# Graph attention and expert layer on one core: who fetches the 128th source row of every chunk of edges

## The chip, the core and the metric

The kernel runs on one core of one Trainium2 chip. Its engines are TensorE (PE, with its weight loads shown apart as PEld), VectorE (DVE), ScalarE (ACT), GpSimd (POOL) and SyncE (SP); SP only waits, loads registers and issues DMAs. The metric is the time of the whole program on the device in microseconds (us), as the median of a few runs.

## The reference, cut to what matters

6250 nodes with 256 features, 206,250 edges sorted by destination. A graph attention layer is followed by a mixture of 16 experts, of which two are chosen per node. The change touches only the part that works edge by edge:

```python
z = einsum('ni,hid->nhd', h, W)                  # 4 heads of 64
e = leaky_relu(es[src] + ed[dst])                # one number per edge and head
ex = exp(e - m[dst])
alpha = ex / segment_sum(ex, dst)[dst]
out = segment_sum(alpha[:, :, None] * z[src], dst)
x = x + out;  x = x + moe(layernorm(x))
```

For each edge the row `z[src]` must be fetched: 256 values and 4 scores `es`, 260 floats or 1040 bytes.

## The kernel before, in words

A first stage writes `z_table` (one row of 260 floats per node) to HBM. The edge stage then goes through the edges in **chunks** of 128 (one edge per partition) and **groups** of `G = 4` chunks: 403 groups. A group lies in one slot of `ring`, which has `RING = 4` slots. A **visit** is a pair of a group and a tile of 128 destination nodes that occurs in it. There are 451 visits, 48 more than groups, so 48 groups have two visits and 355 have one.

- **GpSimd** (`gather`) waits for a group until its slot is free, then issues one indirect DMA per chunk: 128 rows of `z_table`, chosen by a column of `src_idx`, into the 128 partitions of the slot. "Free" means that VectorE has made the message of the last visit of the group four before: `pool.wait_ge(b_msg, done + 1)`, where `group_free` holds the number `done` for each group.
- **SyncE** goes through the groups in order. `relay(g, ...)` waits until group g has landed and raises `b_group` by one; only then may ScalarE open the group. For odd g `replace_pair` loads two more rows of destination numbers (`dst_bc`), and for even g `relay_pair` passes on that such a pair has landed. In the time that is left SyncE gathers whole chunks by itself: `fetch_row` loads one index into a register and copies one row of `z_table` into `side`, 4 rows after an even group and 3 after an odd one (`HAND_ROWS`); when 128 are there, `place_side` copies them into the ring. In this way 10 chunks of 1612 come past GpSimd, which issues 1602 gathers.
- **ScalarE** copies the scores out of the ring when the group is released (`es_edge`, in `open_group`), and makes the exponents.
- **VectorE** makes arguments, one-hot matrices and messages, in an order written out by hand. The number behind each piece says how many visits it lags:

```python
written_out(VISITS, SR, [(e_sum, AHEAD), (look_up, AHEAD + 1), (e_add, AHEAD), (make_ST, 0), (e_lrelu, AHEAD),
                         (accumulate, AHEAD + 1 + MSG_TO_ACC), (e_shift, AHEAD), (one_hot, AHEAD + 1),
                         (e_clamp, AHEAD), (message, AHEAD + 1), (finish, None)], steps=FINISH)
```

In one step VectorE therefore begins visit v with `e_add`, which needs `es_edge` of visit v, and at the end of the same step makes the message of visit v - 1 (`message`, which reads the ring and raises `b_msg`).
- **TensorE** multiplies messages with the one-hot matrices and sums them by destination.

All waits of an engine block what is queued behind them on that engine.

Of the kernel before, what the change touches and what calls it, by code (L numbers as in the profile page):

```python
# [35 lines left out]
P = 128  # L36
G = 4
RING = 4
# [15 lines left out]
ZR = 12  # L54
SOON = AHEAD + 1
SLACK = 4
HAND_ROWS = (4, 3)
LADDER = 4


# [51 lines left out]
def gnn_moe_kernel(nc, E, x, x_turned, src_cols, dst_cols, dst_flat, dst_last, W, a_src, a_dst, gate_w, gate_b, w1, b1, w2, b2, gamma, beta, out):  # L112
    N, D = out.shape
    HEADS, DH = a_src.shape
    EXPERTS, _, F = w1.shape
    TOP = 2
    NT = -(-N // P)
# [3 lines left out]
    ROW = D + HEADS  # L121
    CHUNKS = -(-E // P)
    GROUPS = -(-CHUNKS // G)
# [14 lines left out]
    z_table = nc.dram_tensor("z_table", [NT * P, ROW], F32).ap()  # L138
# [19 lines left out]
    with whole:  # L158
# [27 lines left out]
        src_idx = sb(graph, "src_idx", [P, BLOCKS * P], I32)  # L186
# [381 lines left out]
        b_landed = [sem(f"b_landed{i}") for i in range(RING)]  # L568
        b_over = sem("b_over"); b_go = sem("b_go")
        b_pstep = sem("b_pstep"); b_nodes = sem("b_nodes")  # L570
        b_group = sem("b_group")
        PAIRED, PAIRS = ROWS // 2, -(-GROUPS // 2)
        b_side = [sem(f"b_side{i}") for i in range(2)]; b_placed = sem("b_placed")
        b_dst = [sem(f"b_dst{i}") for i in range(PAIRED)]; b_rows = sem("b_rows")
        b_S = sem("b_S"); b_ST = sem("b_ST")
        b_dest = sem("b_dest"); b_estep = sem("b_estep"); b_arg = sem("b_arg"); b_p = sem("b_p")
# [22 lines left out]
        for batches in SPANS:  # L599
            at = range(BATCHES[batches[0]].start, BATCHES[batches[-1]].stop)  # L600
            assert at.start // KEPT == (at.stop - 1) // KEPT
        SH = 2 * HEADS
        PER_PASS = (b_pstep, b_nodes, b_group, *b_side, b_placed, *b_dst, b_rows, b_S, b_ST, b_dest, b_estep, b_arg, b_p, b_msg, b_sum, b_acc, b_es, b_fstep, b_reset, b_rden,
                    b_scaled, b_added, b_stats, b_var, b_root, b_ready, b_xn, b_xT_ps, b_xT, b_log_ps, b_log, *b_saved)
        assert sorted(one.num for one in PER_PASS) == list(range(b_pstep.num, b_saved[-1].num + 1))
        PASS_STEPS = 11
        HAND_GROUPS, brought, hand_rows = [], 0, {}
        for g in range(GROUPS - RING):
            hand_rows[g] = [divmod(brought + u, P) for u in range(HAND_ROWS[g % 2])]
            brought += HAND_ROWS[g % 2]  # L610
            if brought // P > len(HAND_GROUPS):
                HAND_GROUPS.append(g + RING)
        BY_HAND = {g: m for m, g in enumerate(HAND_GROUPS)}
        THIRDS = 3
        SPAN_TILES = [range(BATCHES[batches[0]].start, BATCHES[batches[-1]].stop) for batches in SPANS]
        PAIRED_SPANS = sum(len(batches) == 2 for batches in SPANS)
# [7 lines left out]
        with ExitStack() as ctx:  # L624
# [12 lines left out]
            earg = sb(ctx, "earg", [P, 4, 3, G * HEADS])  # L637
            msg = sb(ctx, "msg", [P, MR, G, ROW])
            nodes_rest = msg[:, 0, :, :].rearrange("p g c -> p (g c)")[:, 0:NT * SH].rearrange("p (t c) -> p t c", c=SH)
            side = sb(ctx, "side", [P, 2, ROW])  # L640
            psE = [ps(ctx, f"psEb{i}") for i in range(SR // BANKED)]
            psM = [ps(ctx, f"psMb{i}") for i in range(2)]
            psP = [ps(ctx, f"psPb{i}") for i in range(2)]
# [16 lines left out]
            @block.sync  # L660
            def _(sp):
                npass = sp.value_load(npass_i[0:1, 0:1], min_val=1, max_val=PASSES_MAX)
                with sp.Fori(0, npass) as k:
                    def gathered(s, upto):
                        return sum(G - (h in BY_HAND) for h in range(s, upto, RING))

                    def relay(g, s, r):

                        sp.wait_ge(b_landed[s], 16 * (k * gathered(s, GROUPS) + gathered(s, g + 1)))
                        if g in BY_HAND:  # L670
                            sp.wait_ge(b_placed, 16 * (BY_HAND[g] + 1))
                        sp.nop().then_inc(b_group, 1)  # L672

                    def load_pair(g, at):
                        sp.dma_start(dst_bc[:, 2 * at:2 * at + 2, :].rearrange("p o f -> p (o f)"),
                                     over(dst_rows[bass.ds(g * (G * P), 2 * G * P)].unsqueeze(0), [P, 2 * G * P])).then_inc(b_dst[at], 16)

                    def replace_pair(g, at):

                        done = sp.value_load(group_free[0:1, g + 1 - ROWS + RING:g + 2 - ROWS + RING], min_val=1, max_val=VISITS)  # L680
                        sp.wait_ge(b_ST, done)
                        load_pair(g, at)

                    def relay_pair(at, r):
                        sp.wait_ge(b_dst[at], 16 * (r + 1))
                        sp.nop().then_inc(b_rows, 1)
                    def fetch_row(m, p):

                        chunk = HAND_GROUPS[m] * G + G - 1
                        row = sp.value_load(src_idx[p:p + 1, chunk:chunk + 1]).with_bounds(min_val=0, max_val=NT * P - 1)  # L690
                        sp.dma_start(side[p:p + 1, m % 2, :], z_table[bass.ds(row, 1), :]).then_inc(b_side[m % 2], 16)

                    def place_side(g, m):

                        sp.wait_ge(b_side[m % 2], 16 * P * (m // 2 + 1))
                        done = sp.value_load(group_free[0:1, g:g + 1], min_val=0, max_val=VISITS)
                        sp.wait_ge(b_msg, done + 1)
                        sp.dma_start(ring[:, g % RING, G - 1, :], side[:, m % 2, :]).then_inc(b_placed, 16)
                    for at in range(PAIRED):
                        load_pair(2 * at, at)  # L700
                    for at in range(PAIRED - 1):
                        relay_pair(at, 0)

                    for g in range(GROUPS):
                        pair = g // 2 + PAIRED - 1
                        if g % 2 == 0 and pair < PAIRS:
                            relay_pair(pair % PAIRED, pair // PAIRED)
                        relay(g, g % RING, g // RING)
                        if g % 2 and g // 2 + PAIRED < PAIRS:
                            replace_pair(g + ROWS - 1, g // 2 % PAIRED)  # L710
                        if g + 2 in BY_HAND:
                            place_side(g + 2, BY_HAND[g + 2])
                        for m, p in hand_rows.get(g, ()):
                            if m < len(HAND_GROUPS):
                                fetch_row(m, p)

                    for at in range(PAIRED):
                        sp.wait_ge(b_dst[at], 16 * len(range(at, PAIRS, PAIRED)))
                    for i in range(2):
                        sp.wait_ge(b_side[i], 16 * P * len(range(i, len(HAND_GROUPS), 2)))  # L720
                    sp.wait_ge(b_placed, 16 * len(HAND_GROUPS))
                    for done, total in ((b_group, GROUPS), (b_rows, PAIRS), (b_S, VISITS), (b_ST, VISITS), (b_dest, VISITS), (b_estep, 4 * VISITS),
                                        (b_arg, VISITS), (b_p, VISITS), (b_msg, VISITS + 1), (b_sum, VISITS), (b_acc, VISITS), (b_es, VISITS),
                                        (b_fstep, FIN_STEPS), (b_reset, NT), (b_rden, NB), (b_scaled, NT), (b_added, NT), (b_stats, NT), (b_var, len(SPANS)),
                                        (b_root, len(SPANS)), (b_ready, len(SPANS)), (b_xn, NT), (b_xT_ps, NT), (b_xT, NT), (b_log_ps, NT), (b_log, NT),
                                        *((b_saved[i], 16 * len(range(i, NT, XN))) for i in range(XN)), (b_pstep, PASS_STEPS), (b_nodes, 1)):
                        sp.wait_ge(done, total)
                    sp.wait_ge(b_over, 4 * k + 4)
                    sp.sem_inc(apart, 1)
                    sp.sem_clear(range(b_pstep.num, b_saved[-1].num + 1))  # L730
                    sp.sem_inc(b_go, 1)

            @block.gpsimd
            def _(pool):
                npass = pool.value_load(npass_i[0:1, 0:1], min_val=1, max_val=PASSES_MAX)
                with pool.Fori(0, npass) as k:
                    def gather(g, s, r):

                        done = pool.value_load(group_free[0:1, bass.ds(g, 1)], min_val=0, max_val=VISITS)
                        pool.wait_ge(b_msg, done + 1)  # L740
                        pool.sem_inc(apart, 1)
                        for c in range(G - 1 if g in BY_HAND else G):
                            at = src_idx[:, g * G + c:g * G + c + 1]
                            nc.gpsimd.indirect_dma_start(ring[:, s, c, :], None, z_table,  # L744
                                                         bass.IndirectOffsetOnAxis(ap=at, axis=0)).then_inc(b_landed[s], 16)
                    for g in range(GROUPS):
                        gather(g, g % RING, g // RING)
                    pool.drain()
                    pool.sem_inc(b_over, 1)
                    pool.wait_ge(b_go, k + 1)  # L750
# [817 lines left out]
```

## Time and profile before

| | us |
|---|---|
| median of 3 runs (2661.21 to 2662.76) | 2661.33 |
| span of the profiled execution, first to last instruction | 2659.8 |
| median of the runs less that span | 1.5 |
| first release of a group to the last (403 releases) | 88.5 to 2094.5 |
| first gather of the edge stage to the last (1602) | 81.5 to 2091.3 |

The profiled execution has no time of its own apart from its span; 1.5 us is what the median of the runs is longer. The edge stage takes about three quarters of the span. In the rows below "L744" is line 744 of the kernel before, a letter q behind an engine ("SPq") is its instruction queue, and the idle time of a group of instructions is that of its engine just before them, with what ended it.

### The profile page before, as it was taken

The numbers are of one execution on the slowest core, as the hardware profiler recorded it, in microseconds if no ns is written. First come the engines' busy times: TensorE is split into PE (matmuls) and PEld (weight loads), VectorE is DVE, ScalarE is ACT, GpSimd is POOL, SyncE is SP. The second block draws the span as 40 slices with busy tenths as digits, with TensorE's granted clock in tenths as the row PEclk, the third lists the DMA queues.
The fourth block names the chain that finished last, engine by engine and source line by source line (L and its number), as shares of the span: only waits on it lengthen the run. The fifth ranks groups of instructions, "written<-read, shape, count | busy, mean of one in ns | idle before, by whom it ended". The sixth has DMA issues, their size and how long they took to land. (4 is left out here: it accounts for less than half of the span.)

```text
span 2659.8 us, 56988 instructions
## 1 busy us (share of the span) xinstructions
PE 1833.5 (69%) x9023; PEld 1427.5 (54%) x9024; DVE 1783.6 (67%) x5444; ACT 783.4 (29%) x3130; POOL 1810.8 (68%) x1943
## 2 busy tenths in 40 slices
PE   7566766665666666666666666666665449999987
PEld 5344544444454454445444444444454339999985
DVE  6577777777786777767777777676777774333326
ACT  4434112212121221122121212111222235555557
POOL 0577777777777777777777777777777345555547
PEclk9688787888887887878788887887888769999998
DMA  9454545555455554455445555554555328433328
GB/s 318 143 136 132 138 136 140 142 136 140 139 141 138 136 144 136 133 144 140 133 137 142 138 138 139 138 140 134 140 141 138 86 64 248 153 105 108 106 96 282
DMA packets 186615, 380.07 MB, mean 143 GB/s; under 512 B 40053, under 2 KB 90656, under 8 KB 185930
## 3 DMA queue, kind: packets, MB, share of 16 engines
q0 software_dynamic: 87264, 241.69, 33.2%
q1 hardware_dynamic: 76152, 114.56, 14.0%
q10 hardware_dynamic: 22898, 20.85, 2.8%
q14 instruction: 239, 1.96, 0.2%
q8 instruction: 62, 1.02, 0.2%
HBM read 341.68 MB, written 33.93 MB: 141 GB/s over the span
## 5 line engine op out<-in xcount | busy, mean ns | idle before, releaser
L744 POOL DMA_INDIRECT ring<-z_table,src_idx x1602 | 1518.8, 948 | 497.6 <-issue 475.7
L1032 PE MATMUL psMb<-msg,S 128*128 128x260 f32 x3608 | 1183.7, 484 | 529.2 <-DVE msg L904 528.7
L1032 PEld LDWEIGHTS psMb<-msg,S 128*128 128x128 f32 x3608 | 812.4, 236 | 712.4 <-DVE msg L904 571.0
L904 DVE TENSOR_TENSOR msg<-ring,psPb 128x1024 f32<-128x1024 f32 x451 | 546.1, 1211 | 0.0
L952 ACT COPY es_edge<-ring 128x16 f32 x451 | 91.5, 203 | 1387.1 <-SPq L672 1347.5
L816 DVE TENSOR_TENSOR earg<-es_edge,dest_sum 128x16 f32<-128x16 f32 x451 | 80.5, 178 | 380.8 <-ACT es_edge L952 346.4
L804 DVE TENSOR_TENSOR S<-iota_f,psPb 128x512 f32<-128x512 f32 x451 | 306.2, 679 | 1.7 <-ACT psPb L961 1.6
L1021 PEld LDWEIGHTS psEb<-node_thirds,ST 128*128 128x128 bf16 x1804 | 104.6, 105 | 322.9 <-issue 300.0
L798 DVE TENSOR_SCALAR ST<-dst_bc,iota_p 128x512 bf16 x451 | 170.6, 378 | 130.5 <-issue 124.4
L1021 PE MATMUL psEb<-node_thirds,ST 128*128 x1804 | 120.8, 179 | 187.7 <-DVE earg L833 96.1
L1396 DVE COPY xT<-psXd 128x256 f32<-128x256 f32 x108 | 45.9, 425 | 263.9 <-PE psXd L1330 263.9
L1308 POOL DMA_INDIRECT rows_sb<-norm_rows,src_sb x108 | 108.2, 1002 | 161.4 <-DVE src_sb L1385 145.5
L1340 PE MATMUL psHd<-xT,w_sb 128*128 128x128 f32 x1728 | 212.5, 277 | 0.0
L1352 PE MATMUL psYd<-w_all,hid 128*128 x864 | 204.3, 379 | 0.3 <-ACT hid L1375 0.3
L1340 PEld LDWEIGHTS psHd<-xT,w_sb 128*128 128x128 f32 x1728 | 203.5, 193 | 0.1
L921 DVE TENSOR_TENSOR acc<-acc,psMb 128x260 f32 x451 | 190.9, 423 | 8.6 <-issue 5.2
L1352 PEld LDWEIGHTS psYd<-w_all,hid 128*128 128x128 f32 x864 | 155.9, 190 | 17.3 <-issue 0.5
L1363 ACT COPY w_sb<-w_all 128x1024 f32 x108 | 112.8, 1045 | 151.2 <-PE psHd L1340 129.8
L1315 POOL DMA_INDIRECT pair_rows<-y_sb,dst_sb x108 | 106.7, 988 | 45.6 <-issue 33.8
L1375 ACT ACTIVATE hid<-psHd,b1T 128x128 f32<-128x128 f32 x432 | 123.6, 368 | 30.2 <-issue 26.2
L941 ACT ACTIVATE psPb<-dst_col,visit_base 128x4 f32 x451 | 120.3, 267 | 1.6 <-issue 1.6
L810 DVE TENSOR_REDUCE dest_sum<-psEb 128x32 f32<-128x96 f32 x451 | 111.8, 248 | 2.2 <-DVE shift_b L882 1.1
(214 smaller groups left out, 1578.7 us busy)
## 6 DMA issues: line engine op xcount, KB each, us to landing
dst_bc<-dst_rows SPq DMA_DIRECT2D x202, 256.0 KB, 3.4
ring<-z_table,src_idx POOLq DMA_INDIRECT x1602
side<-z_table SPq DMA_DIRECT2D x1280, 1.0 KB
w_all<-in_L_ffn_w_dram SPq DMA_DIRECT2D x32, 512.0 KB, 5.4
b_sb<-in_L_ffn_b_dram ACTq DMA_DIRECT2D x108, 128.0 KB, 3.1
got<-pair_rows SPq DMA_DIRECT2D x48, 256.0 KB, 4.1
z_table<-z_out SPq DMA_DIRECT2D x49, 130.0 KB, 6.3
norm_rows<-xnb ACTq DMA_DIRECT2D x49, 128.0 KB, 2.6
```

The source lines that it names most:

```text
L744: nc.gpsimd.indirect_dma_start(ring[:, s, c, :], None, z_table, bass.IndirectOffsetOnAxis(ap=at, axis=0)).then_inc(b_landed[s], 16)
L798: nc.vector.tensor_scalar(ST[:, s % MR, :], dst_bc[:, bass.ds(slot, 1), :].rearrange("p o f -> p (o f)"), iota_p[:, 0:1], None, ALU.is_equ ...
L804: nc.vector.tensor_tensor(S[:, s % MR, :, :], over(iota_f[:, 0:P].unsqueeze(1), [P, G, P]), over(psP[s % 2][:, G * HEADS:G * HEADS + G].un ...
L904: nc.vector.tensor_tensor(msg[:, s % MR, :, 0:D].rearrange("p g (h d) -> p g h d", h=HEADS), ring[:, bass.ds(slot, 1), :, 0:D].rearrange(" ...
L921: nc.vector.tensor_tensor(at, at, psM[s % 2][:, 0:ROW], ALU.add).then_inc(b_acc, 1)
L941: nc.scalar.activation(psP[s % 2][:, G * HEADS:G * HEADS + G], dst_col[:, bass.ds(group * G, G)], ACT.Identity, bias=visit_base[:, v:v + 1])
L1021: last = nc.tensor.matmul(dest_of(s)[:, c * THIRDS * SH:(c + 1) * THIRDS * SH], ST[:, s % MR, c * P:(c + 1) * P], node_thirds[:, bass.ds(t ...
L1032: last = nc.tensor.matmul(psM[s % 2][:, 0:ROW], S[:, s % MR, c, :], msg[:, s % MR, c, :], start=c == 0, stop=c == G - 1)
L1340: last = nc.tensor.matmul(psH[s % 2][:, f * P:(f + 1) * P], w1_sb[:, s % 2, c, f * P:(f + 1) * P], xT[:, s % 2, c, :], start=c == 0, stop= ...
L1352: last = nc.tensor.matmul(psY[s % 2][:, 0:D], hid[:, s % 2, f, :], w2_f, start=f == 0, stop=f == FC - 1)
L1363: nc.scalar.copy(w1_sb[:, s % 2, :, :].rearrange("p c f -> p (c f)"), w_all[:, bass.ds(e, 1), 0:KD * F].rearrange("p o f -> p (o f)")).the ...
L1375: last = nc.scalar.activation(hid[:, s % 2, f, :], psH[s % 2][:, f * P:(f + 1) * P], ACT.Relu, bias=b1T[:, bass.ds(e, 1), f:f + 1].rearran ...
```

## The change

GpSimd now gathers the first 127 rows of every chunk and SyncE copies the last row of every chunk straight into partition 127 of the ring. For that, `bring_rows(g, s)` loads the four indices of a group with one register load, waits for the slot as GpSimd does, and issues four DMAs of one row each. It is called for groups 0 to 2 ahead of the loop and for group g + 3 behind the release of group g. The buffer `side`, `fetch_row`, `place_side` and the ten chunks brought by hand are gone, so GpSimd issues all 1612 gathers. The release of a group now waits for both.

```diff
-HAND_ROWS = (4, 3)
+TAKEN = P - 1
...
                     def relay(g, s, r):
-                        sp.wait_ge(b_landed[s], 16 * (k * gathered(s, GROUPS) + gathered(s, g + 1)))
-                        if g in BY_HAND:
-                            sp.wait_ge(b_placed, 16 * (BY_HAND[g] + 1))
+                        sp.wait_ge(b_landed[s], 16 * G * (k * len(range(s, GROUPS, RING)) + r + 1))
+                        sp.wait_ge(b_brought[s], 16 * G * (r + 1))
                         sp.nop().then_inc(b_group, 1)
...
-                    def fetch_row(m, p):
-                        chunk = HAND_GROUPS[m] * G + G - 1
-                        row = sp.value_load(src_idx[p:p + 1, chunk:chunk + 1]).with_bounds(min_val=0, max_val=NT * P - 1)
-                        sp.dma_start(side[p:p + 1, m % 2, :], z_table[bass.ds(row, 1), :]).then_inc(b_side[m % 2], 16)
-                    def place_side(g, m):
-                        sp.wait_ge(b_side[m % 2], 16 * P * (m // 2 + 1))
+                    def bring_rows(g, s):
                         done = sp.value_load(group_free[0:1, g:g + 1], min_val=0, max_val=VISITS)
+                        _, loaded = nc.values_load_multi_w_load_instructions(src_idx[TAKEN:P, g * G:(g + 1) * G], engines=[mybir.EngineType.SP])
+                        rows = [row.with_bounds(min_val=0, max_val=NT * P - 1) for row in loaded]
                         sp.wait_ge(b_msg, done + 1)
-                        sp.dma_start(ring[:, g % RING, G - 1, :], side[:, m % 2, :]).then_inc(b_placed, 16)
+                        for c in range(G):
+                            sp.dma_start(ring[TAKEN:P, s, c, :], z_table[bass.ds(rows[c], 1), :]).then_inc(b_brought[s], 16)
...
+                    for g in range(RING - 1):
+                        bring_rows(g, g)
                     for g in range(GROUPS):
...
                         relay(g, g % RING, g // RING)
                         if g % 2 and g // 2 + PAIRED < PAIRS:
                             replace_pair(g + ROWS - 1, g // 2 % PAIRED)
-                        if g + 2 in BY_HAND:
-                            place_side(g + 2, BY_HAND[g + 2])
-                        for m, p in hand_rows.get(g, ()):
-                            if m < len(HAND_GROUPS):
-                                fetch_row(m, p)
+                        if g + RING - 1 < GROUPS:
+                            bring_rows(g + RING - 1, (g + RING - 1) % RING)
...
-                        for c in range(G - 1 if g in BY_HAND else G):
-                            at = src_idx[:, g * G + c:g * G + c + 1]
-                            nc.gpsimd.indirect_dma_start(ring[:, s, c, :], None, z_table,
+                        for c in range(G):
+                            at = src_idx[0:TAKEN, g * G + c:g * G + c + 1]
+                            nc.gpsimd.indirect_dma_start(ring[0:TAKEN, s, c, :], None, z_table,
                                                          bass.IndirectOffsetOnAxis(ap=at, axis=0)).then_inc(b_landed[s], 16)
```

On SyncE, this is what stood behind the release of an odd group early in the edge stage: register arithmetic for the release (L669), the load of a pair of destination rows (L680, L675), and then one register load (L690) and one DMA (L691) for each row brought by hand, of which the first two of three are shown.

```order
L669 ISA
L680 TENSOR_LOAD group_free
L680 ISA x2
L675 DMA dst_bc<-dst_rows 128x1024
L690 TENSOR_LOAD src_idx
L691 ISA
L691 DMA side<-z_table 1x260
L690 TENSOR_LOAD src_idx
L691 ISA
L691 DMA side<-z_table 1x260
```

Now the same place reads as follows: L668 and L663 are the pair of destination rows, L678 loads the number that frees the slot, L679 loads four indices, the first L683 carries the wait for the message, and a DMA of one row follows each L683 (two of four are shown).

```order
L668 TENSOR_LOAD group_free
L668 ISA x2
L663 DMA dst_bc<-dst_rows 128x1024
L678 TENSOR_LOAD group_free
L678 ISA x2
L679 TENSOR_LOAD src_idx
L681 REGISTER_ALU
L683 ISA
L683 DMA ring<-z_table 1x260
L683 ISA
L683 DMA ring<-z_table 1x260
```

Three register loads for indices have become one, the copies go to the ring and not to the side buffer, and a wait on VectorE's messages now stands on SyncE between the release of one group and the release of the next.

On GpSimd a group was, in its wait for the slot (L739, L740) and its gathers (L744):

```order
L739 TENSOR_LOAD group_free
L739 ISA x2
L740 REGISTER_ALU
L744 DMA ring<-z_table,src_idx 128x260 x4
```

and is now:

```order
L722 TENSOR_LOAD group_free
L722 ISA x2
L723 REGISTER_ALU
L727 DMA ring<-z_table,src_idx 127x260 x4
```

Nothing moved there; the gathers have 127 partitions in place of 128, and the ten groups that had three gathers have four.

## Rows read from the trace of the kernel before

**Rows 1.** The page: busy time of each engine, share of span, instructions.
```profile
PE 1833.5 (69%) x9023; PEld 1427.5 (54%) x9024; DVE 1783.6 (67%) x5444; ACT 783.4 (29%) x3130; POOL 1810.8 (68%) x1943
```

**Rows 2.** Busy time by engine in the edge stage, granted clock, DMA share, GB/s.
```profile
90.00:2090.00 2000.00, 1286.70 (x5648) 949.52 (x5648) 1475.27 (x4373) 432.62 (x2282) 1510.25 (x1594) 0.82 0.51 138
```

**Rows 3.** Groups by line: busy us, mean ns, then idle before and releasers.
```profile
L744 POOL DMA_INDIRECT ring<-z_table,src_idx x1602 | 1518.8, 948 | 497.6 <-issue 475.7 <-DVE msg L904 21.9
...
L952 ACT COPY es_edge<-ring 128x16 f32 x451 | 91.5, 203 | 1387.1 <-SPq L672 1347.5
```

**Rows 4.** Who waited for whom: us in total, times, longest.
```profile
ACT es_edge L952 <- SPq L672: 1347.5, 375, 6.5
...
POOL ring L744 <- DVE msg L904: 21.9, 68, 0.9
```

**Rows 5.** SyncE's own waits, same columns.
```profile
SPq L672 <- DMA ring<-z_table,src_idx: 385.9, 357, 5.4
```

**Rows 6.** Single lines: ns min/median/max, first and last start; the last near 1006 us.
```profile
L744 POOL DMA_INDIRECT ring<-z_table,src_idx x1602: 940/946/1382, 81.5 to 2091.3; - x178
...
L904 DVE TENSOR_TENSOR msg<-ring,psPb x451: 1204/1212/1217, 96.5 to 2098.7; 128x1024 f32<-128x1024 f32 x151
...
L672 SPq EVENT_SEMAPHORE  x403: 17/17/28, 88.5 to 2094.5; - x135
...
L672 SPq EVENT_SEMAPHORE  x1: 17/17/17, 1006.3 to 1006.3; - x1
```

**Rows 7.** Timeline from 1000 to 1016 us: start, us, engine, line, idle before.
```profile
1000.52 1.21 DVE L904 TENSOR_TENSOR msg<-ring,psPb 128x1024 f32<-128x1024 f32 x1
...
1004.05 1.22 DVE L904 TENSOR_TENSOR msg<-ring,psPb 128x1024 f32<-128x1024 f32 x1
...
1006.47 0.20 ACT L952 COPY es_edge<-ring 128x16 f32 x1 [4.71 <-SPq L672]
...
1008.13 3.15 SPq L691 DMA_DIRECT2D side<-z_table  x4
...
1008.68 1.21 DVE L904 TENSOR_TENSOR msg<-ring,psPb 128x1024 f32<-128x1024 f32 x1
...
1010.93 0.95 POOL L744 DMA_INDIRECT ring<-z_table,src_idx  x1 [0.30 <-issue]
1011.62 0.20 ACT L952 COPY es_edge<-ring 128x16 f32 x1 [2.51 <-SPq L672]
...
1012.18 0.95 POOL L744 DMA_INDIRECT ring<-z_table,src_idx  x1 [0.30 <-issue]
1012.22 0.35 SPq L675 DMA_DIRECT2D dst_bc<-dst_rows  x1
...
1013.91 1.21 DVE L904 TENSOR_TENSOR msg<-ring,psPb 128x1024 f32<-128x1024 f32 x1
```

**Rows 8.** SyncE's instructions for one row by hand: ns min/median/max, first and last.
```profile
L690 SPq TENSOR_LOAD <-src_idx x1280: 267/499/782, 88.5 to 1910.9; - x183
...
L691 SPq FUSED_REGOPS  x1280: 37/37/47, 88.9 to 1911.5; - x183
L691 SPq MOVE side<-z_table x1280: 29/29/40, 88.9 to 1911.6; - x183
L691 SPq DMA_DIRECT2D side<-z_table x1280: 254/258/327, 89.0 to 1911.6; - x183
```

**Rows 9.** GpSimd's DMA queue (packets, MB, share of 16 engines); its other users.
```profile
q0 software_dynamic: 87264, 241.69, 33.2%
...
L1308 POOL DMA_INDIRECT rows_sb<-norm_rows,src_sb x108 | 108.2, 1002 | 161.4 <-DVE src_sb L1385 145.5
...
L1315 POOL DMA_INDIRECT pair_rows<-y_sb,dst_sb x108 | 106.7, 988 | 45.6 <-issue 33.8
```

**Rows 10.** Timeline at the start of the edge stage: SyncE's DMAs back to back.
```profile
79.64 1.75 SPq L675 DMA_DIRECT2D dst_bc<-dst_rows  x4
```

**Rows 11.** DMA issues by line: KB each, median us to landing.
```profile
dst_bc<-dst_rows SPq DMA_DIRECT2D x202, 256.0 KB, 3.4
```

More of the change, by code:

```diff
@@ L572, in gnn_moe_kernel @@
         PAIRED, PAIRS = ROWS // 2, -(-GROUPS // 2)
-        b_side = [sem(f"b_side{i}") for i in range(2)]; b_placed = sem("b_placed")
+        b_brought = [sem(f"b_brought{i}") for i in range(RING)]
         b_dst = [sem(f"b_dst{i}") for i in range(PAIRED)]; b_rows = sem("b_rows")
@@ L602, in gnn_moe_kernel @@
         SH = 2 * HEADS
-        PER_PASS = (b_pstep, b_nodes, b_group, *b_side, b_placed, *b_dst, b_rows, b_S, b_ST, b_dest, b_estep, b_arg, b_p, b_msg, b_sum, b_acc, b_es, b_fstep, b_reset, b_rden,
+        PER_PASS = (b_pstep, b_nodes, b_group, *b_brought, *b_dst, b_rows, b_S, b_ST, b_dest, b_estep, b_arg, b_p, b_msg, b_sum, b_acc, b_es, b_fstep, b_reset, b_rden,
                     b_scaled, b_added, b_stats, b_var, b_root, b_ready, b_xn, b_xT_ps, b_xT, b_log_ps, b_log, *b_saved)
@@ L606, in gnn_moe_kernel @@
         PASS_STEPS = 11
[L607 to L613, printed above, removed]
         THIRDS = 3
@@ L639, in gnn_moe_kernel @@
             nodes_rest = msg[:, 0, :, :].rearrange("p g c -> p (g c)")[:, 0:NT * SH].rearrange("p (t c) -> p t c", c=SH)
-            side = sb(ctx, "side", [P, 2, ROW])
             psE = [ps(ctx, f"psEb{i}") for i in range(SR // BANKED)]
@@ L663, in _ @@
                 with sp.Fori(0, npass) as k:
-                    def gathered(s, upto):
-                        return sum(G - (h in BY_HAND) for h in range(s, upto, RING))
                     def relay(g, s, r):
-                        sp.wait_ge(b_landed[s], 16 * (k * gathered(s, GROUPS) + gathered(s, g + 1)))
-                        if g in BY_HAND:
-                            sp.wait_ge(b_placed, 16 * (BY_HAND[g] + 1))
+                        sp.wait_ge(b_landed[s], 16 * G * (k * len(range(s, GROUPS, RING)) + r + 1))
+                        sp.wait_ge(b_brought[s], 16 * G * (r + 1))
                         sp.nop().then_inc(b_group, 1)
@@ L710, in _ @@
                             replace_pair(g + ROWS - 1, g // 2 % PAIRED)
-                        if g + 2 in BY_HAND:
-                            place_side(g + 2, BY_HAND[g + 2])
-                        for m, p in hand_rows.get(g, ()):
-                            if m < len(HAND_GROUPS):
-                                fetch_row(m, p)
+                        if g + RING - 1 < GROUPS:
+                            bring_rows(g + RING - 1, (g + RING - 1) % RING)
                     for at in range(PAIRED):
                         sp.wait_ge(b_dst[at], 16 * len(range(at, PAIRS, PAIRED)))
-                    for i in range(2):
-                        sp.wait_ge(b_side[i], 16 * P * len(range(i, len(HAND_GROUPS), 2)))
-                    sp.wait_ge(b_placed, 16 * len(HAND_GROUPS))
+                    for s in range(RING):
+                        sp.wait_ge(b_brought[s], 16 * G * len(range(s, GROUPS, RING)))
                     for done, total in ((b_group, GROUPS), (b_rows, PAIRS), (b_S, VISITS), (b_ST, VISITS), (b_dest, VISITS), (b_estep, 4 * VISITS),
```

## The prediction

> **What bounds the kernel now.** I read the page first [rows 1]: no engine is busy for more than 69% of the span, so the bound has to be looked for by stage. In the 2000 us of the edge stage [rows 2] GpSimd is busy for 1510 us, VectorE for 1475, TensorE for 1287; DMA engines stand at half. The groups by line [rows 3] then say what GpSimd's remaining time is: 475.7 us of "issue" before 1602 gathers, about 0.30 us each, against only 21.9 us in which it waited for VectorE to free a slot (68 times, [rows 4]). A gather is 0.948 us plus these 0.30, and the timeline shows two of them starting 1.25 us apart with nothing else between them [rows 7]. So GpSimd runs at its own pace: (2091.3 - 81.5) / 1601 = 1.255 us per gather, and the releases keep the same pace, (2094.5 - 88.5) / 402 = 4.99 us per group [rows 6].
>
> Everybody behind it waits: ScalarE spent 1347.5 us waiting for SyncE's release [rows 4], and SyncE in turn 385.9 us for a gather to land [rows 5], about 1 us per group. SyncE is thus idle for only a fifth of each group; it is no bound, but not far from one.
>
> The timeline [rows 7] gives the fact on which my forecast rests. A group is released at 1006.3 [rows 6]; `es_edge` starts at 1006.47; VectorE, which needs it, begins its step, and the message at the end of that step ends at 1008.68 + 1.21 = 1009.89. By the written order this is the message of the *previous* visit, the last one of the group before. Start of `es_edge` to end of message is 3.42 us; for the next group 1011.62 to 1015.12, or 3.50. Hence slot of group g - 1 is freed some 3.6 us **after** group g has been released. For GpSimd this is harmless, since it asks for that slot much later.
>
> **The change, part by part.**
>
> *GpSimd.* Ten gathers more: 10 x 1.255 = 12.6 us if GpSimd stayed the bound. The price of a gather with 127 rows is in no row. Bounds: the three indirect transfers here, all with 128 rows, take 0.948, 0.988 and 1.002 us [rows 3, 9], so I take 0.95, with nothing gained for one row less (one 128th of 0.948 us is 7 ns, or 12 us in all, which would just cancel the ten). How a different row count might change more than this is a rival below.
>
> *Transfers removed.* 1280 rows into `side`, ten copies from it, and their register loads leave SyncE. They stood in the time in which SyncE would have waited for the gathers, so taking them away gains nothing by itself.
>
> *SyncE's new work per group.* Two register loads (0.5 us each by [rows 8]) plus, for odd groups, the pair of destination rows (0.35 us and a load) come right behind the release. That is 1.4 to 2.5 us and is hidden, since the wait that follows ends 3.6 us behind the release. The pair's own wait, on the one-hot matrix of a visit that runs five visits ahead, is long met.
>
> *The new wait.* `bring_rows(g + 3)` stands behind the release of g and waits for the message of the last visit of g - 1. As just read, that message cannot end before about 3.6 us after this very release. Behind the wait on SyncE's queue stand four DMAs and then the release of g + 1, for which ScalarE and VectorE wait. Thus release, score copy, VectorE's step, four DMAs and next release form a closed loop, which runs once per group and does not depend on GpSimd.
>
> *The price of four DMAs.* In before, four rows by hand took 3.15 us from first to last DMA [rows 7]: (3.15 - 0.258) / 3 = 0.964 us per row, of which 0.499 is the load [rows 8]. DMA, arithmetic and move are 0.258 + 0.037 + 0.029 = 0.324; the remaining 0.141 is the hand-over between four instructions, 0.035 each. Without the load a row costs 0.324 + 3 x 0.035 = 0.43, and four cost 1.73 us. Bounds: if arithmetic and move hid under the DMA, 4 x (0.258 + 0.035) = 1.17; if a DMA straight behind another took the 0.35 us of the larger one [rows 7], 4 x (0.35 + 0.17) = 2.1. Four larger ones back to back took 1.75 us [rows 10], which also speaks for the middle.
>
> *The loop.* Release to `es_edge` 1006.3 to 1006.47: 0.17. `es_edge` to end of message: 3.43. Message to SyncE: estimated as 0.10, between nothing and the 0.17 of the other hand-over. Four rows: 1.73. The two waits of the release: 0.10, estimated as three of the 0.035 hand-overs. Sum: 5.53 us, against 4.99 now.
>
> *Groups with two visits.* There VectorE makes one step with no release in front of it and the next while SyncE's four DMAs are already done. Two unstalled messages are 1004.05 - 1000.52 = 3.53 us apart [rows 7], so such a group costs 2 x 3.53 = 7.06 us.
>
> *The stage.* 402 intervals between releases, 48 of them with two visits: 354 x 5.53 + 48 x 7.06 = 1957.6 + 338.9 = 2296.5 us. Before: 2094.5 - 88.5 = 2006.0. Difference +290.5. Ahead of the loop SyncE brings three groups, each about two loads with their hand-overs and four rows, 1.0 + 0.2 + 1.73 = 2.9 us. It does so behind three pairs of destination rows, the third of which is issued at some 80.9 [rows 10] and lands 3.4 us later [rows 11]: 84.3 + 8.7 = 93.0 for the first release in place of 88.5, +5. Nothing behind the stage changes. The profiled execution would have 2659.8 + 296 = 2956 us; the median of the runs lies 1.5 above its span, which gives **2957**.
>
> *A rule against 127 rows.* Rows first: GpSimd's queue had its packets on the engines for 33.2% of 16 engines' span [rows 9]. Over 1602 + 108 + 108 transfers that is 0.332 x 16 x 2659.8 / 1818 = 7.8 us of one engine per transfer, or 0.49 us if 16 share it. The Trainium skill, DMA: Bandwidth & Descriptors, section "Why a DMA increments its semaphore by 16 and not by 1", says that a DMA is spread over the largest number up to 16 that divides its slowest dimension, which for 127 partitions is 1, though it also tells of software-issued direct copies on trn2 that were still spread over all 16. By the exception the sum stays as it is. By the rule each gather is one engine's work; no run here shows which holds for an indirect one.
>
> **The rivals.**
>
> 1. *Gathers of 127 rows become the bound.* If each lies on one engine, it lands 7.8 us behind its descriptors. From the freeing of a slot: 3 x 1.255 + 0.95 + 7.8 = 12.5 us until the group is there; the loop wants it at 0.10 + 1.73 + 0.10 + 2 x 5.53 = 13.0 us behind the same point. So even this is just hidden, and from 8.3 us per transfer on it decides. At twice 7.8 us, say because two gathers queue on one engine, three groups take 0.95 + 3.77 + 15.6 + 3.6 = 23.9 us, 8.0 per group, and the kernel 2661 + 402 x (8.0 - 4.99) = 3870. Likewise if a gather with its issue costs GpSimd more than 2296 / 1612 = 1.42 us. Against it: half of the DMA time is free [rows 2]. Chance of a time over 3100: 0.11. (The rule of the Trainium skill named above, DMA: Bandwidth & Descriptors, would bring this about.)
> 2. *The four DMAs cost less back to back,* 1.17 us: the loop is 4.97, the stage 354 x 4.97 + 339 = 2098, the kernel 2661 + 92 + 5 = 2758. For it: only 0.258 us of each row is the DMA [rows 8]. Chance of a time from 2670 to 2800: 0.10, most of it (0.08) at 2740 and above.
> 3. *Faster.* A gather of 127 rows takes a cheaper path through GpSimd and the loop doesn't hold SyncE. If a gather's 0.95 halved, 1612 x (0.47 + 0.30) = 1241 us, and VectorE with 451 x 3.53 = 1592 us would be the bound: 2661 - 2006 + 1592 = 2247. It decides only if four rows cost under 0.91 us: with 48 x 7.06 taken off, 2006 leaves 1667 / 354 = 4.71 us for a loop, less 3.43 + 0.37. Their DMAs alone, 4 x 0.258, are more than that. Chance 0.04, and 0.02 for a time within 0.2%, where the wait costs nothing and the ten gathers and one row less cancel.
>
> **How the numbers follow.** My forecast has 0.73. Its own range takes the bounds of four rows: 1.17 gives 2758; 2.1 gives a loop of 5.90 and 2957 + 354 x 0.37 = 3088; the low end is rival 2, so its own range is 2800 to 3090. The range for all reaches down over most of rival 2 and up to the bound, 2740 to 3100: it leaves out rival 1 (0.11), the rest of rival 2 (0.02) and rival 3 with its neighbour (0.06), 0.19 in all. Faster by over 0.2% (about what a measurement of this kernel tells from no change) 0.04; within 0.2%, 0.02; slower 0.94.
>
> **What would show it.** Right: ScalarE's wait for the release grows to some 1640 us; SyncE waits for VectorE's message behind nearly every release and hardly for a landing; releases are 5.5 us apart, 7 in two-visit groups; GpSimd waits for the message before most groups; a row's DMA starts 0.43 us behind the one before. Wrong: SyncE's wait is still for landing gathers, or a gather takes over 1.1 us (rival 1); rows 0.3 us apart (rival 2); a message that is there when SyncE asks for it (rival 3).

## The result, and the profile after

The changed kernel takes 5268.33 us (median of 4 runs, 5266.59 to 5272.02) against 2662.05 us for the kernel before: a ratio of 1.979, 95% interval 1.977 to 1.982. That is far outside the range of the prediction, in the direction that it gave.

The page of the changed kernel: busy time of the engines, then two of the groups by line (busy us, mean ns, idle before, releasers).

```profile
PE 2328.8 (44%) x9023; PEld 1704.4 (32%) x9024; DVE 1851.6 (35%) x5444; ACT 782.0 (15%) x3130; POOL 4404.6 (84%) x1953
...
L727 POOL DMA_INDIRECT ring<-z_table,src_idx x1612 | 4112.6, 2551 | 503.0 <-issue 480.1
...
L935 ACT COPY es_edge<-ring 128x16 f32 x451 | 91.8, 203 | 4028.9 <-SPq L660 4006.3
```

GpSimd went from 1811 us [rows 1] to 4405, and one line holds all of it: a gather takes 2551 ns in place of 948 [rows 3]. The idle time before it, 0.31 us each, is what it was. The same lines one by one (ns min/median/max, first and last start), with the landing of the gathers' DMAs as the last line of the first view:

```profile
L727 POOL DMA_INDIRECT ring<-z_table,src_idx x1612: 2544/2548/2899, 80.6 to 4687.9; - x180
L683 SPq DMA_DIRECT2D ring<-z_table x1612: 224/228/1426, 85.8 to 4670.1; - x180
...
DMA to landing us min/median/max: 7.8/8.0/11.4
```

```profile
L660 SPq EVENT_SEMAPHORE  x403: 27/28/28, 100.0 to 4698.1; - x135
```

The minimum, 2544 ns, stands next to the median: every gather is slow, not some. Nor is it a queue that has filled up, since the first gather, with none in front of it, is slow already:

```profile
80.59 2.90 POOL L727 DMA_INDIRECT ring<-z_table,src_idx  x1 [5.76 <-issue]
```

From first to last gather there are 1611 x 2.860 = 4607.3 us, where [rows 6] had 2009.8. This is +2597.5; the last release comes 10.2 us after the last gather and not 3.2 (+7.0); the first gather starts 0.9 earlier. Together +2603.6, and the spans differ by 5264.7 - 2659.8 = 2604.9. Nothing else moved the time.

The DMA queue of GpSimd (packets, MB, share of 16 engines) tells what a gather has become:

```profile
q0 software_dynamic: 861504, 253.62, 25.0%
```

Before, 87264 packets [rows 9] were 48 for each of 1818 transfers, 3 per engine if all 16 have the same number. Take 216 later transfers at 48 off: (861504 - 10368) / 1612 = 528 packets for a gather of 127 rows, 33 per engine, although there is one row less to move. The bytes grew by only 5%.

SyncE's own waits (us in total, times, longest):

```profile
SPq L660 <- DMA ring<-z_table,src_idx: 1928.1, 403, 11.4
SPq L683 <- DVE msg L887: 617.4, 399, 4.8
```

SyncE does wait for VectorE's message behind nearly each release, as forecast, but then for each group another 4.8 us for the gathers. The timeline (start, us, engine, line, idle before) shows why the first wait costs nothing here:

```profile
2004.57 2.54 POOL L727 DMA_INDIRECT ring<-z_table,src_idx  x1 [0.30 <-issue]
2007.42 2.55 POOL L727 DMA_INDIRECT ring<-z_table,src_idx  x1 [0.31 <-issue]
2009.68 0.20 ACT L935 COPY es_edge<-ring 128x16 f32 x1 [10.70 <-SPq L660]
...
2010.27 2.55 POOL L727 DMA_INDIRECT ring<-z_table,src_idx  x1 [0.30 <-issue]
...
2011.82 0.99 DVE L816 TENSOR_SCALAR earg<-earg 128x16 f32<-128x16 f32 x1
2011.90 1.21 DVE L887 TENSOR_TENSOR msg<-ring,psPb 128x1024 f32<-128x1024 f32 x1
...
2013.12 2.55 POOL L727 DMA_INDIRECT ring<-z_table,src_idx  x1 [0.30 <-DVE msg L887]
...
2013.29 2.08 SPq L683 DMA_DIRECT2D ring<-z_table  x4
...
2021.44 0.20 ACT L935 COPY es_edge<-ring 128x16 f32 x1 [11.16 <-SPq L660]
```

Gathers stand back to back, 2.85 us apart, four of them 11.4 us. SyncE has its four rows out at 2015.4, some 5.7 us behind the opening of the group at 2009.68, and then waits until 2021 for the next landing.

### The profile page after: what moved, and what is told of

It is laid out like the page before. It is cut to its first block and busy times, and to the rows that moved or that the text cites. A ratio compares the mean times of both kernels' runs of the same rounds, so it can differ in the third digit from the quotient of the medians.

```text
span 5264.7 us, 58524 instructions
## 1 busy us (share of the span) xinstructions
PE 2328.8 (44%) x9023; PEld 1704.4 (32%) x9024; DVE 1851.6 (35%) x5444; ACT 782.0 (15%) x3130; POOL 4404.6 (84%) x1953
## 3 DMA queue, kind: packets, MB, share of 16 engines
q0 software_dynamic: 861504, 253.62, 25.0%
q8 instruction: 62, 1.02, 0.1%
## 5 line engine op out<-in xcount | busy, mean ns | idle before, releaser
L727 POOL DMA_INDIRECT ring<-z_table,src_idx x1612 | 4112.6, 2551 | 503.0 <-issue 480.1
L1015 PE MATMUL psMb<-msg,S 128*128 128x260 f32 x3608 | 1635.8, 631 | 669.6 <-DVE msg L887 668.4
L1015 PEld LDWEIGHTS psMb<-msg,S 128*128 128x128 f32 x3608 | 1096.3, 318 | 954.7 <-DVE msg L887 705.9
L1004 PEld LDWEIGHTS psEb<-node_thirds,ST 128*128 128x128 bf16 x1804 | 88.6, 108 | 2219.2 <-issue 2215.1
L887 DVE TENSOR_TENSOR msg<-ring,psPb 128x1024 f32<-128x1024 f32 x451 | 573.0, 1271 | 0.0
L816 DVE TENSOR_SCALAR earg<-earg 128x16 f32<-128x16 f32 x451 | 508.6, 1128 | 0.0
L781 DVE TENSOR_SCALAR ST<-dst_bc,iota_p 128x512 bf16 x451 | 212.6, 472 | 129.7 <-issue 128.7
L1025 PE MATMUL psTb<-gate,xnTb 128*128 128x16 f32 x196 | 46.1, 354 | 191.4 <-ACT xnTb L985 191.4
L793 DVE TENSOR_REDUCE dest_sum<-psEb 128x32 f32<-128x96 f32 x451 | 128.3, 285 | 2.7 <-DVE shift_b L865 1.3
```

What stands on the lines that cost most here:

```text
L727: nc.gpsimd.indirect_dma_start(ring[0:TAKEN, s, c, :], None, z_table, bass.IndirectOffsetOnAxis(ap=at, axis=0)).then_inc(b_landed[s], 16)
L781: nc.vector.tensor_scalar(ST[:, s % MR, :], dst_bc[:, bass.ds(slot, 1), :].rearrange("p o f -> p (o f)"), iota_p[:, 0:1], None, ALU.is_equ ...
L793: nc.vector.tensor_reduce(dest_sum[:, s % 4, :, :], dest_of(s).rearrange("p (g k c) -> p g c k", g=G, k=THIRDS), AX.X, ALU.add).then_inc(b ...
L816: nc.vector.tensor_scalar(earg[:, s % 4, 0, :], earg[:, s % 4, 2, :], 0.0, None, ALU.min).then_inc(b_arg, 1)
L887: nc.vector.tensor_tensor(msg[:, s % MR, :, 0:D].rearrange("p g (h d) -> p g h d", h=HEADS), ring[:, bass.ds(slot, 1), :, 0:D].rearrange(" ...
L1004: last = nc.tensor.matmul(dest_of(s)[:, c * THIRDS * SH:(c + 1) * THIRDS * SH], ST[:, s % MR, c * P:(c + 1) * P], node_thirds[:, bass.ds(t ...
```

## The experiments

Theory A: a gather of 127 rows is dear by itself, since 127 can't be shared out evenly among the DMA engines. Theory B: SyncE's rows disturb the gathers. Theories C and D, on which counts are dear, stand with the second run. A further question was whether the loop of the forecast exists at all, since the changed kernel hides it. Each of the first five runs has one time, beside 2660.57 us for the kernel before in the first four and 2664.22 in the fifth.

**127 rows alone.** SyncE's part is taken out, on the changed kernel:

```diff
                     def relay(g, s, r):
-                        sp.wait_ge(b_brought[s], 16 * G * (r + 1))
...
-                    for g in range(RING - 1):
-                        bring_rows(g, g)
...
-                        if g + RING - 1 < GROUPS:
-                            bring_rows(g + RING - 1, (g + RING - 1) % RING)
...
             def _(pool):
+                nc.gpsimd.memset(ring[:, :, :, :], 0.0).then_inc(b_zero, 1)
```

> The changed kernel without SyncE's part: GpSimd gathers 127 rows per chunk, nobody fetches the last row (partition 127 of the ring is cleared once and stays zero), so one edge in 128 is left out. Theory A (the gather of 127 rows is dear by itself, because 127 has no divisor that spreads it over the DMA engines): a gather still takes about 2.55 us plus 0.30, 1612 x 2.86 = 4610 us between first and last, and the kernel 5260 to 5275, some 5 us more for the clearing. Theory B (SyncE's single rows, on the same engines and the same ring, slow the gathers): the gather falls back to about 0.95, and the kernel to 2661 + 12.6 + 5 = 2680.

Measured: 5268.67 us. The row of the gathers by line:

```profile
L722 POOL DMA_INDIRECT ring<-z_table,src_idx x1612 | 4116.3, 2554 | 497.5 <-issue 474.3 <-DVE msg L882 23.2
```

2554 ns with no row of SyncE anywhere: B is out. The page's row for GpSimd's queue is the same as that of the changed kernel, so the packets too come with the gathers:

```profile
q0 software_dynamic: 861504, 253.62, 25.0%
```

**The price by row count.** On the kernel of the run above:

```diff
-                            at = src_idx[0:TAKEN, g * G + c:g * G + c + 1]
-                            nc.gpsimd.indirect_dma_start(ring[0:TAKEN, s, c, :], None, z_table,
-                                                         bass.IndirectOffsetOnAxis(ap=at, axis=0)).then_inc(b_landed[s], 16)
+                            kind = (g * G + c) % len(KINDS)
+                            KINDS[kind](g * G + c, ring[:, s, c, :]).then_inc(b_landed[s], 16)
```

> As the run with 127 rows alone, but the chunks take turns with 128, 127, 126, 125, 124, 122, 121, 113, 112 and 64 rows, each count from a line of its own, the rest of the ring zero: it leaves those edges out and measures the price by row count. Theory A (price goes with the rows that the busiest engine gets, n divided by the largest divisor of n up to 16; through 0.946 us at 8 and 2.548 at 127 this is 0.838 + 0.0135 per row): 128 0.95, 127 2.55, 126 (9 rows) 0.96, 125 (25) 1.18, 124 (31) 1.26, 122 (61) 1.66, 121 (11) 0.99, 113 (113) 2.36, 112 (7) 0.93, 64 (4) 0.89; mean 1.37 + 0.30, kernel 2661 - 2010 + 1612 x 1.67 = 3350. Theory C (anything but all 128 partitions is slow): every count but 128 near 2.5, kernel near 5000. Theory D (odd counts are slow, even ones not): 127, 125, 121 and 113 near 2.5, the others at or under 0.95, kernel near 3700.

Measured: 3431.34 us. Groups by line; the lines are 127 rows (L725), 113 (L749), 122 (L741), 124 (L737), 125 (L733), 121 (L745), 126 (L729), 128 (L721), 112 (L753) and 64 (L757):

```profile
L725 POOL DMA_INDIRECT ring<-z_table,src_idx x162 | 412.6, 2547 | 49.4 <-issue 49.4
L749 POOL DMA_INDIRECT ring<-z_table,src_idx x161 | 381.1, 2367 | 49.1 <-issue 49.1
L741 POOL DMA_INDIRECT ring<-z_table,src_idx x161 | 267.6, 1662 | 49.0 <-issue 43.2 <-DVE msg L927 5.8
L737 POOL DMA_INDIRECT ring<-z_table,src_idx x161 | 209.0, 1298 | 54.5 <-issue 50.5 <-DVE msg L927 3.9
L733 POOL DMA_INDIRECT ring<-z_table,src_idx x161 | 194.5, 1208 | 49.0 <-issue 49.0
L745 POOL DMA_INDIRECT ring<-z_table,src_idx x161 | 162.2, 1007 | 52.0 <-issue 51.2 <-DVE msg L927 0.8
L729 POOL DMA_INDIRECT ring<-z_table,src_idx x161 | 158.7, 985 | 49.1 <-issue 45.4 <-DVE msg L927 3.7
L721 POOL DMA_INDIRECT ring<-z_table,src_idx x162 | 156.4, 965 | 88.0 <-DVE msg L927 67.7 <-issue 17.8 <-DVEq L783 2.6
L753 POOL DMA_INDIRECT ring<-z_table,src_idx x161 | 150.3, 933 | 49.1 <-issue 48.8 <-DVE msg L927 0.3
L757 POOL DMA_INDIRECT ring<-z_table,src_idx x161 | 145.8, 905 | 49.1 <-issue 49.1
```

| rows n | largest divisor k up to 16 | n / k | expected, us | measured, us |
|---|---|---|---|---|
| 127 | 1 | 127 | 2.55 | 2.547 |
| 113 | 1 | 113 | 2.36 | 2.367 |
| 122 | 2 | 61 | 1.66 | 1.662 |
| 124 | 4 | 31 | 1.26 | 1.298 |
| 125 | 5 | 25 | 1.18 | 1.208 |
| 121 | 11 | 11 | 0.99 | 1.007 |
| 126 | 14 | 9 | 0.96 | 0.985 |
| 128 | 16 | 8 | 0.95 | 0.965 |
| 112 | 16 | 7 | 0.93 | 0.933 |
| 64 | 16 | 4 | 0.89 | 0.905 |

A holds for all ten within 0.04 us; its line was drawn through 128 and 127, so the other eight are its test. C (anything short of 128) fails with 126, 112 and 64; D (odd counts) with 121, which is odd and cheap, and 122, which is even and dear. The kernel's time came out 81 us over the expected 3350 (whose own sum gives 3343): the gathers' mean is 1.388 us, not 1.37, some 30 us in all, and the idle time before them is 538 us and not 1612 x 0.30 = 484, because 82 us of waits for messages came in, 68 of them before 128.

The Trainium skill, DMA: Bandwidth & Descriptors, section "Why a DMA increments its semaphore by 16 and not by 1", gives that divisor as the number of engines that a DMA runs on; the ten rows agree with it, for an indirect gather, and its exception for some direct copies does not show here. That GpSimd's own time for a gather goes with n / k stands in these rows.

The packets follow n / k too. Suppose that the rows of the busiest engine go four to a packet, that one packet more closes its share, and that each of the 16 engines gets as many packets as the busiest: then a gather makes 16 x (n / k / 4, rounded up, + 1) packets, 48 for 128 rows and 528 for 127. Over the ten counts of this run, with the 10368 packets of the later transfers, that is 302032, and the page has exactly this:

```profile
q0 software_dynamic: 302032, 226.60, 27.8%
```

**Rows beside the ring,** which runs the forecast's loop with gathers of 128 rows:

```diff
-                            sp.dma_start(ring[TAKEN:P, s, c, :], z_table[bass.ds(rows[c], 1), :]).then_inc(b_brought[s], 16)
+                            sp.dma_start(beside[TAKEN - c:P - c, g % (RING - 1), :], z_table[bass.ds(rows[c], 1), :]).then_inc(b_brought[s], 16)
...
-                            at = src_idx[0:TAKEN, g * G + c:g * G + c + 1]
-                            nc.gpsimd.indirect_dma_start(ring[0:TAKEN, s, c, :], None, z_table,
+                            at = src_idx[:, g * G + c:g * G + c + 1]
+                            nc.gpsimd.indirect_dma_start(ring[:, s, c, :], None, z_table,
```

> All 128 rows are gathered by GpSimd as before, and SyncE's four rows per group stay with their wait and their place in the order, but go to a small buffer beside the ring that nobody reads; nothing is left out. It runs the loop of the forecast (release, step of VectorE, four DMAs, next release) without the gathers of 127 rows. If the forecast had the loop right: releases about 5.5 us apart, GpSimd waiting for messages, kernel 2880 to 2990. If the wait costs nothing: ten more gathers alone, 2661 + 12.6 = 2674.

Measured: 2975.55 us. Waits of all engines (two rows) and of SyncE in the edge stage (two), and its releases:

```profile
ACT es_edge L936 <- SPq L661: 1739.6, 390, 6.8
...
POOL ring L728 <- DVE msg L888: 343.1, 299, 3.6
```

```profile
SPq L684 <- DVE msg L888: 818.4, 399, 5.0
...
SPq L661 <- DMA ring<-z_table,src_idx: 6.0, 1, 6.0
```

```profile
L661 SPq EVENT_SEMAPHORE  x403: 27/28/28, 92.7 to 2406.8; - x135
```

GpSimd now waits for messages 343 us, not 22 [rows 4], and SyncE for a gather only once. The releases take (2406.8 - 92.7) / 402 = 5.76 us each; the forecast's 2296.5 / 402 were 5.71.

**The same, one group earlier.** Only the place of the rows changes:

```diff
-                        if g + RING - 1 < GROUPS:
-                            bring_rows(g + RING - 1, (g + RING - 1) % RING)
+                        if g + RING - 2 < GROUPS:
+                            bring_rows(g + RING - 2, (g + RING - 2) % RING)
```

> As the run with the rows beside the ring, with one difference: behind the release of group g SyncE brings the rows of group g + 2 and not g + 3, so it waits for a message that belongs to a group two before and is made before that release. If the loop is what costs in the other run: the wait is gone and the kernel falls to 2661 + 12.6 = 2674, give or take 8. If SyncE's work itself (loads and DMAs) costs: as in the other run.

Measured: 2677.78 us. SyncE's waits in the edge stage are for landings again, and of 818.4 us for messages 8.4 are left:

```profile
SPq L661 <- DMA ring<-z_table,src_idx: 483.3, 391, 5.5
...
SPq L684 <- DVE msg L888: 8.4, 12, 1.5
```

Same loads, same DMAs, 298 us less: the cost was a wait, in front of the next release, for a message that is made only behind the last one, and not SyncE's work.

**126 rows on GpSimd, two per chunk on SyncE.** One size of the changed kernel:

```diff
-TAKEN = P - 1
+TAKEN = P - 2
...
+                        for p in range(TAKEN, P):
                             for c in range(G):
-                            sp.dma_start(ring[TAKEN:P, s, c, :], z_table[bass.ds(rows[c], 1), :]).then_inc(b_brought[s], 16)
+                                sp.dma_start(ring[p:p + 1, s, c, :], z_table[bass.ds(rows[p][c], 1), :]).then_inc(b_brought[s], 16)
```

> The changed kernel with one size changed: GpSimd gathers 126 rows of each chunk and SyncE brings the last two, eight rows per group, with two register loads; nothing is left out. Theory A (127 rows are dear because they can't be spread; 126 can): a gather takes 0.98 us as in the run by row counts, so GpSimd no longer bounds, and the loop of the forecast does, with eight DMAs at the 0.41 us that rows took back to back: 3.43 + 0.17 + 0.10 + 8 x 0.41 + 0.10 = 7.1 us per group, 354 x 7.1 + 48 x 7.3 = 2864, kernel 2661 - 2006 + 2864 + 8 = 3525, although it moves more rows to SyncE than the changed kernel at 5268. Rival (any count short of 128 that leaves rows to SyncE is slow through SyncE's rows): slower than 5268, since there are twice as many.

Measured: 3569.77 us, with twice the rows on SyncE 1699 us *faster* than the changed kernel. The gathers by line, SyncE's wait in the edge stage, and GpSimd's queue:

```profile
L730 POOL DMA_INDIRECT ring<-z_table,src_idx x1612 | 1612.3, 1000 | 1309.3 <-DVE msg L890 914.3 <-issue 394.9
```

```profile
SPq L686 <- DVE msg L890: 593.8, 399, 3.0
```

```profile
q0 software_dynamic: 113536, 239.78, 26.1%
```

A gather is 1.00 us, and GpSimd waits 914 us for messages, as SyncE does behind nearly every release: the loop with eight DMAs holds both, within 45 us of the expected time. The packets are 64 for a gather of 126 rows, (113536 - 10368) / 1612, as the sum by n / k has it: 16 x (9 / 4, rounded up, + 1).

**Three tries to beat the kernel before.** What stayed of the change is that one register load can bring four indices. The first two use it for whole groups by hand:

```diff
-                        chunk = HAND_GROUPS[m] * G + G - 1
-                        row = sp.value_load(src_idx[p:p + 1, chunk:chunk + 1]).with_bounds(min_val=0, max_val=NT * P - 1)
-                        sp.dma_start(side[p:p + 1, m % 2, :], z_table[bass.ds(row, 1), :]).then_inc(b_side[m % 2], 16)
+                        first = HAND_GROUPS[m] * G
+                        _, loaded = nc.values_load_multi_w_load_instructions(src_idx[p:p + 1, first:first + G], engines=[mybir.EngineType.SP])
+                        for c in range(G):
+                            row = loaded[c].with_bounds(min_val=0, max_val=NT * P - 1)
+                            sp.dma_start(side[p:p + 1, c, :], z_table[bass.ds(row, 1), :]).then_inc(b_side[m % 2], 16)
```

> The kernel before, with the one part of the change that the runs showed to be cheap, four indices per register load: SyncE brings whole groups (four chunks, 128 x 4 rows) into a side buffer, seven rows per group on average (HAND_QUADS 2, 1, 2, 2), and copies each in one DMA; GpSimd keeps gathers of 128 rows and skips five groups, 20 chunks in place of 10. If GpSimd stays the bound: ten gathers fewer, 10 x 1.255 = 12.6 us, 2649 (ratio 0.9953). If SyncE becomes the bound (7/4 x (0.6 + 4 x 0.41) + 0.7 = 4.6 us of 5.0 per group, so it is near): same or slower.

> The same with six rows per group on average (HAND_QUADS 2, 1, 2, 1), four groups or 16 chunks brought by SyncE. If GpSimd is the bound in both: 6 x 1.255 = 7.5 us less than before, 2654 (ratio 0.9972), 5 us more than with five groups. If SyncE is too busy in the run with five: this one is the faster of the two.

Measured: five groups 2677.17 us, ratio 1.0055 (1.0041 to 1.0069); four groups 2666.28 us, ratio 1.0013 (1.0004 to 1.0022). Neither gained, and four came out faster than five, as expected if SyncE is too busy with five. SyncE's waits for landings, with five groups and then with four:

```profile
SPq L676 <- DMA ring<-z_table,src_idx: 142.4, 126, 7.4
```

```profile
SPq L676 <- DMA ring<-z_table,src_idx: 309.4, 244, 5.7
```

With four groups GpSimd's gathers by line, and those behind a skipped group in the timeline, are these:

```profile
L750 POOL DMA_INDIRECT ring<-z_table,src_idx x1596 | 1514.6, 949 | 506.9 <-issue 469.2 <-DVE msg L911 37.8
```

```profile
522.58 0.95 POOL L750 DMA_INDIRECT ring<-z_table,src_idx  x1 [0.30 <-issue]
525.11 0.95 POOL L750 DMA_INDIRECT ring<-z_table,src_idx  x1 [1.58 <-DVE msg L911]
...
531.02 0.94 POOL L750 DMA_INDIRECT ring<-z_table,src_idx  x1 [1.19 <-DVE msg L911]
```

GpSimd gets ahead by four gathers and then waits for slots, 37.8 us in all where [rows 4] had 21.9: here it idles 1.58 and 1.19 us where 0.30 is usual, so that within 9 us some 2.2 of the 5.0 us of four gathers at 1.25 are given back. The timeline has such idle times behind the other three skipped groups too (3.02; 1.98 and 1.97; 1.55 and 1.02 us). Over the usual 0.30 that makes 10 us in all, more than the 7.5 that were to be won. The third try takes the four indices from four groups, two apart, so that one gather is skipped at a time:

```diff
-                        row = sp.value_load(src_idx[p:p + 1, chunk:chunk + 1]).with_bounds(min_val=0, max_val=NT * P - 1)
+                        _, loaded = nc.values_load_multi_w_load_instructions(src_idx[p:p + 1, chunk:chunk + (SETS - 1) * STRIDE * G + 1:STRIDE * G],
+                                                                             engines=[mybir.EngineType.SP])
```

> As the runs with whole groups by hand, but SyncE's four indices of one register load belong to the last chunks of four groups that lie two apart, so that GpSimd skips one gather in each of 16 groups and not four in a row; six rows per group on average (HAND_QUADS 2, 1, 2, 1), 16 chunks by hand in place of 10. If the whole groups lost their gain because GpSimd, four gathers ahead at once, ran into slots not yet free (the waits for messages behind a skipped group): this one keeps it, 6 x 1.255 = 7.5 us less than before, 2654 to 2658 (ratio 0.997 to 0.998). If they lost it because SyncE's longer bursts release groups late: no faster than before.

Measured: 2721.95 us, ratio 1.0236 (1.0222 to 1.0250). SyncE's register loads in the run with four groups and in this one:

```profile
L694 SPq TENSOR_LOAD <-src_idx x512: 295/484/740, 87.8 to 1833.0; - x171
```

```profile
L694 SPq TENSOR_LOAD <-src_idx x512: 860/1058/1395, 87.6 to 1978.3; - x171
```

Four indices that lie apart take 1.06 us and four neighbours 0.48. The run therefore changed two things, and doesn't tell whether skipping one gather at a time would have kept the gain; that stays open. None of the three beats the kernel before.

## Why the prediction was wrong

1. **The step that failed** is the term "The price of a gather with 127 rows is in no row [...] so I take 0.95, with nothing gained for one row less". It measured 2.55 us: 1612 gathers at 2.86 us with their issue, in place of the 1.25 in the sum. Its two ends, 0.948 and 1.002, were no bounds, since all three rows behind them had 128 partitions: they bounded the price of that shape, and the change was one of shape.
2. **Rival 1** named what happened, with the right point from which it decides (1.42 us for a gather with its issue; 2.86 measured) and the right sign, a gather over 1.1 us, but priced the wrong half of it. The landing on one engine was sized at 7.8 us and is 8.0 from issue to landing; it is indeed hidden, since GpSimd waits for messages 22.9 us in all, as before. That GpSimd's *own time* would go with the rows of the busiest engine, I did not see, and a chance of 0.11 was too little for a price that no row showed and against which a rule stood.
3. **The loop** was right, but is not what bounds the changed kernel; that the kernel came out slower, the forecast got right for another reason, by luck. Alone the loop gives 2975.55 us for a forecast of 2957, releases 5.76 us apart for 5.71, a wait of ScalarE of 1740 us for 1640. Moving the wait one group earlier takes it away. That the sum fits so well is in part chance: in the trace of the run beside the ring four rows took 1.51 us in the median and not 1.73 (their DMA is 0.228 us, not 0.258), and `es_edge` to end of message 3.59 and not 3.43.
4. **The ten gathers more** were put at 12.6 us; the run without the loop is 17.2 us over the kernel before, which is no clear difference, since 15 runs of the kernel before reach from 2661.45 to 2667.47.
5. **Rivals 2 and 3** did not come about: four rows took 1.51 us where rival 2 had 1.17, and the wait is met late behind nearly every release, as the rows of before showed.
6. **Two slips** in the working move nothing: 4 x 0.43 is 1.72 us, not 1.73, and SyncE also waited 99.6 us for rows of destination numbers, so that it was idle for about a quarter of each group and not a fifth.

Of the cause, the runs show that the gather's price comes with its row count, whatever SyncE does, and goes with n / k for ten counts. The packets speak for fillers on the engines without rows, as many as the busiest engine has rows. By size, the 528 of a gather of 127 rows in the trace of the changed kernel are 31 of 4160 bytes and one of 3120 (four rows and three), 465 of 16 bytes and 15 of 12, and 16 of 4. Shared among 15 engines without a row, that is 31 packets of 16 bytes and one of 12 for each, or 127 fillers of 4 bytes; the trace does not name the engine of a packet. That GpSimd's 1.6 us more go into writing these fillers is argued: it fits a price that is linear in n / k, but no run shows what GpSimd does within a gather.

## What to carry to other kernels

A row less can cost more than twice the time: before an indirect gather loses partitions, look for the largest divisor up to 16 of what is left (126, 124 and 121 are not alike), and take a price from rows of the same shape only. A term that no row shows, and that stands 1612 times on the bounding engine, belongs in the range with all its weight, or in a test by itself. And where an engine that releases work also waits for that work's result, look which release the awaited result belongs to; one group earlier was worth 298 us here.

## What the runs showed of the hardware that was not expected

- A gather of 127 rows made 528 packets and 2.55 us of GpSimd, one of 128 rows 48 packets and 0.95.
- VectorE's clamp (`e_clamp`, 16 values per partition) takes 0.17 us in the median before and 1.12 us after. In the timeline above it starts at 2011.82 and ends at 2012.81, when the gather that began at 2010.27 ends (2012.82). So do 449 of the 450 that began within a gather, to 30 ns. The two views by line:

```profile
L833 DVE TENSOR_SCALAR earg<-earg x451: 158/167/415, 94.1 to 2096.6; 128x16 f32<-128x16 f32 x151
```

```profile
L816 DVE TENSOR_SCALAR earg<-earg x451: 167/1117/1727, 103.9 to 4700.2; 128x16 f32<-128x16 f32 x151
```

  The Trainium skill, SBUF — State Buffer, section "Who interferes with whom", says that an operation of VectorE in a two-port mode and GpSimd shut each other out for a whole instruction, whoever comes first. The trace agrees with it in part only, and which mode the clamp runs in no view shows. In the kernel before, the 181 clamps that began in the first 0.5 us of a gather took 0.20 us at most and ended well before it; the 59 that began from 0.55 to 0.75 us behind its start all ended with it. One of the first kind:

```profile
1008.43 0.95 POOL L744 DMA_INDIRECT ring<-z_table,src_idx  x1 [0.30 <-issue]
...
1008.61 0.17 DVE L833 TENSOR_SCALAR earg<-earg 128x16 f32<-128x16 f32 x1
```

  So GpSimd holds the clamp up only from some 0.5 us into a gather, and a longer gather does so for longer. It cost the kernel nothing here: GpSimd waited for messages 22.9 us in all, against 21.9 before [rows 4].
- TensorE's granted clock in the edge stage was 0.59 of full speed, against 0.82 [rows 2], with TensorE busy for 39% of that stage in place of 64%. It lies between the two levels (1.2 and 2.4 GHz), so part of the stage ran at the lower one; a matmul of messages takes 631 ns, not 484. This is off the path too, since GpSimd does not wait for it. The stage after, in the columns of [rows 2]:

```profile
90.00:4690.00 4600.00, 1781.62 (x5648) 1225.92 (x5648) 1543.57 (x4379) 429.80 (x2278) 4103.69 (x1609) 0.59 0.31 62
```

- A register load of four indices on SyncE: 0.48 us for neighbours, 1.06 us for four that lie eight apart.
